# Late branch, one projection for the last head without a block of its own, and the last wavelength on VectorE in every unit but the first

## What is computed

```
for wl in range(16):
    m = cos(phase_modulators[wl])[None, :, None, None]
    scores = einsum('bhqd,bhkd->bhqk', Q * m, K * m) * SCALE
    scores = scores * cos(KERR * scores * scores)
    attn = softmax(scores)
    acc += einsum('bhqk,bhkd->bhqd', attn, V) * interference_weights[wl]
out = x + (acc / 16) @ Wo + bo + experts(layernorm(x))
```

## Time and profile before

| | us |
|---|---|
| median of 3 runs (lowest, highest) | 1777.92 (1775.83, 1778.24) |
| the profiled execution: its own time | 1777.68 |
| the profiled execution: span, first to last instruction | 1776.0 |
| ScalarE busy in the span | 1717.8 (97%) |
| VectorE busy | 1506.6 (85%) |
| TensorE matmuls busy | 1488.9 (84%) |

### The profile page before, as it was taken

How to read it: one execution, slowest core, us unless ns; L and a number is a source line. 1 busy time by engine, 2 the same in 40 slices (tenths; PEclk the granted TensorE clock), 3 DMA queues, 4 the chain that set the end, 5 groups by cost and what they waited for, 6 DMA issues and landing times. The chain is left out here.

```text
span 1776.0 us, 45925 instructions
## 1 busy us (share of the span) xinstructions
PE 1488.9 (84%) x20120; PEld 955.6 (54%) x20120; DVE 1506.6 (85%) x2397; ACT 1717.8 (97%) x524; POOL 166.1 (9%) x184
## 2 busy tenths in 40 slices
PE   5978888887788899999999988878778778778877
PEld 4545555554455566666666655555445545445555
DVE  4555778888988999999999988899998888898784
ACT  3899999999999999999999999999999999999995
POOL 4404000111110000000000000123320000000000
PEclk8999999999999999999999999999999999999999
DMA  3200000110001111011110000000000000000001
GB/s 121 99 15 16 16 5 29 61 43 24 26 9 36 36 43 44 15 33 41 43 43 22 16 18 8 24 25 26 26 21 2 15 15 15 15 15 2 8 13 32
DMA packets 45566, 49.57 MB, mean 28 GB/s; under 512 B 7436, under 2 KB 38068, under 8 KB 45364
## 3 DMA queue, kind: packets, MB, share of 16 engines
q1 hardware_dynamic: 41920, 42.04, 7.4%
q0 software_dynamic: 2048, 4.20, 0.8%
q10 hardware_dynamic: 1396, 0.33, 0.1%
HBM read 30.44 MB, written 15.73 MB: 26 GB/s over the span
## 5 line engine op out<-in xcount | busy, mean ns | idle before, releaser
L1298 ACT ACTIVATE Pr<-T 128x4096 f32<-128x4096 f32 x479 | 1682.6, 3659 | 10.4 <-PE bank L1169 6.6
L1169 PE MATMUL bank<-Pr,Vst 128*32 128x256 f32 x15392 | 932.8, 382 | 257.8 <-ACT Pr L1298 141.3
L1169 PEld LDWEIGHTS bank<-Pr,Vst 128*32 128x32 f32 x15392 | 520.8, 109 | 553.0 <-issue 351.9
L1110 DVE COPY T<-bank 128x512 f32<-128x512 f32 x248 | 168.9, 684 | 73.0 <-PE bank L1104 71.3
L1094 DVE TENSOR_REDUCE negmax<-bank 128x2 f32<-128x512 f32 x248 | 158.6, 679 | 32.9 <-PE bank L1088 32.7
L1262 PE MATMUL bank_b<-terms,ident 128*128 128x128 f32 x1024 | 148.7, 278 | 0.4 <-DVE terms L1250 0.2
L1221 DVE SCALAR_TENSOR_TENSOR shared<-d_mantissa,shared 128x1024 f32<-128x1024 f32 x113 | 142.4, 1260 | 2.6
L1231 DVE TENSOR_SCALAR pv_s<-bank,row_scale 128x512 f32<-128x512 f32 x192 | 142.0, 740 | 0.8 <-PE bank L1169 0.8
L1218 DVE SCALAR_TENSOR_TENSOR shared<-shared,d_scaled 128x1024 f32<-128x1024 f32 x113 | 137.5, 1217 | 0.0
L1215 DVE SCALAR_TENSOR_TENSOR d_mantissa<-d_mantissa 128x1024 f32<-128x1024 f32 x113 | 137.3, 1215 | 0.0
L1262 PEld LDWEIGHTS bank_b<-terms,ident 128*128 128x128 f32 x1024 | 130.0, 191 | 13.5 <-issue 10.7
(11 more groups left out here) (229 smaller groups left out, 900.3 us busy)
## 6 DMA issues: line engine op xcount, KB each, us to landing
Ks<-qk_parts SPq DMA_DIRECT2D x30, 288.0 KB
Qs<-qk_parts SPq DMA_DIRECT2D x90, 96.0 KB
qk_parts<-work SPq DMA_DIRECT2D x12, 384.0 KB, 3.4
work<-in_L_ffn_w_dram SPq DMA_DIRECT2D x16, 256.0 KB, 3.6
dispatched<-d_scaled SPq DMA_DIRECT2D x5, 512.0 KB, 6.4
region<-dispatched SPq DMA_DIRECT2D x8, 320.0 KB, 3.4
expert_out<-work SPq DMA_DIRECT2D x8, 320.0 KB, 2.6
out_dram<-base SPq DMA_DIRECT2D x8, 256.0 KB, 2.2
```

The costliest lines, as they stand in the source:

```text
L1110: nc.vector.tensor_copy(T[par][:, ds(p * BANK, BANK)], sc_bank[rr][:, :]).then_inc(sc_read, 1)
L1169: ins = nc.tensor.matmul(bank[VC * j:VC * (j + 1), half * SEQ:(half + 1) * SEQ], Vst[par][:, at:at + VC], moving, start=opens and half == ...
L1298: nc.scalar.activation(Pr[n % RING][:, :], T[par][:, :], ACT.Exp, scale=scales[u % 2][w]).then_inc(exp_done, 1)
```

## The change

What it does, in four parts.

1. The branch is moved from ahead of `head_*` to after the first scores: normalising, turning, the first Q and K and all of `first_scores` now run ahead of it. The bound uses squares instead of roots, and its operations come later on VectorE and TensorE.
2. Unit 0: one part per step in steps 0 to 3 and two in steps 4 and 5, instead of two ahead of step 0 and two in each of steps 0 to 2; the 16 small matmuls of side 0's gate logits go into four steps; the tiles of unit 1 are scored in steps 6, 7, 9, 10 and transposed 2, 3, 3 in steps 12 to 14.
3. `D_CHUNKS`: four chunks on VectorE in units 1 to 5, where it was 0, 3, 2, 2, 2.
4. The second block is gone. Side 0's heads are projected in unit 30, side 1's first 15 heads (120 rows) in unit 31. The last exp comes in two halves. The last head's 128 x 128 sum, made transposed by exchanging the operands, is multiplied with `spread_rows`, which holds the last 8 rows of `Wo` 16 times on a block diagonal: four matmuls of 512 columns, an add and a store for each.

```diff
-            D_CHUNKS = [{FIRST: 0, NORM: 0, SIDE: 3, ROUTE: 2, QKV: 2, PLAIN: 4, EXPERT: 4, FINAL: 4}[k] for k in KINDS]
+            D_CHUNKS = [{FIRST: 0, NORM: 4, SIDE: 4, ROUTE: 4, QKV: 4, PLAIN: 4, EXPERT: 4, FINAL: 4}[k] for k in KINDS]
...
+            LOGITS0_AT = {(0, 10): 0, (0, 13): 1, (0, 15): 2, (1, 0): 3}
+            PARTS_AT = {0: (0,), 1: (1,), 2: (2,), 3: (3,), 4: (4, 5), 5: (6, 7)}
...
+                if u == 0:
+                    return [(1, 0, p) for p in {6: (0, 1), 7: (2, 3), 9: (4, 5), 10: (6, 7)}.get(w, ())]
...
+                    return [(1, SIDE_B, p) for p in {12: (0, 1), 13: (2, 3, 4), 14: (5, 6, 7)}.get(w, ())]
...
             spread_max(1)
-            pe_v(pe, 1)
             first_transposed(1)
-            pe_v(pe, 2)
-            pe_v(pe, 3)
+            for n in range(1, NQ_SIDE):
+                pe_v(pe, n)
...
+                if (u, w) == LAST_EXP:
+                    for half, signal in enumerate((last_half, exp_done)):
+                        to, src = (t[:, :].rearrange("p (j h k) -> p j h k", j=GR, h=2)[:, :, half, :] for t in (Pr[n % RING], T[par]))
+                        nc.scalar.activation(to, src, ACT.Exp, scale=scales[u % 2][w]).then_inc(signal, 1)
+                    return
...
+            OUT_AT = {(UNITS - 2, 1 + 4 * n + 2 * k): (n, 2 * k) for n in range(NQ_SIDE) for k in range(2)}
+            OUT_AT.update({(UNITS - 1, 5 + 2 * n + k): (NQ_SIDE + n, 2 * k) for n in range(NQ_SIDE) for k in range(2)})
...
+                pe.wait_ge(summed, UNITS)
+                for n in range(NQ_SIDE):
+                    nc.tensor.matmul(last_banks[n][:, :], last_T, spread_rows[:, n * BANK:(n + 1) * BANK], start=True, stop=True).then_inc(o_last, 1)
...
+                sp.wait_ge(spread_room, 1)
+                for j in range(GR):
+                    for q in range(BANK // P):
+                        row, t = (q * GR + j) * HD, q + GR * j
+                        sp.dma_start(spread_rows[row:row + HD, t * D:(t + 1) * D], Wo[D - HD:D, :]).then_inc(rows_spread, 16)
```

More of the change, by code:

```diff
@@ L415, in pre_vector @@
             nc.vector.tensor_copy(flag[:, :], one[:, 1:2]).then_inc(flag_ready, 1)
-        def pre_tensor(pe):
[L418 to L421, removed]
-            ins.then_inc(norms_made, 1)
-            pe.wait_ge(const_ready, 3)
-            pe.wait_ge(bound_ready, 1)
-            nc.tensor.transpose(banks[3][0:1, 0:P], bound[:, 2:3], ident[:, :]).then_inc(bound_turned, 1)
@@ L427, in head_tensor @@
-        def head_tensor(pe):
+            first_max(2)
+            first_max(3)
+            copy_k(3)
+            for b in range(HALF_B, SIDE_B):
+                first_max(b)
+        def pre_tensor(pe):
             def turn_x(n):
@@ L456, in first_scores, with head_tensor @@
                             ins.then_inc(first_made, 1)
+            pe.wait_ge(const_ready, 3)
+            turn_x(0)
+            turn_x(1)
+            pe.wait_ge(first_in, 64)
+            first_qk(0)
+            turn_x(2)
+            pe.wait_ge(w_squared, 2)
+            for i in range(2):
+                ins = nc.tensor.matmul(banks[4][:, i:i + 1], wsq[:, i * D:(i + 1) * D], one_col[:, :], start=True, stop=True)
+            ins.then_inc(norms_made, 1)
+            first_qk(1)
+            first_scores(0)
+            turn_x(3)
+            first_qk(2)
+            pe.wait_ge(bound_ready, 1)
+            first_scores(1)
+            pe.wait_ge(xT_copied, NQ_SIDE)
+            nc.tensor.transpose(banks[6][0:1, 0:P], bound[:, 2:3], ident[:, :]).then_inc(bound_turned, 1)
+            first_qk(3)
+            first_scores(2)
+            first_scores(3)
+        def head_tensor(pe):
             def spread_max(half):
@@ L1148, in pe_products @@
                 pe.wait_ge(v_staged, u + 1)
-                if not shares:
+                if not shares and (u, w) != LAST_EXP:
                     pe.wait_ge(exp_done, EXPS_BEFORE[u] + w + 1)
@@ L1740, in all_general_tensor @@
                     pe_part(pe, m)
-                for i in (GB, LOGITS0):
-                    pe_gate(pe, i)
+                pe_gate(pe, GB)
+                for i in range(4):
+                    pe_logits0(pe, i)
                 for w in range(W):
```

353 lines of the change are left out of this document (177 added, 176 removed).

## The result

The changed kernel is slower: 1786.41 us median of 5 runs (1784.47 to 1789.49) against 1777.5 (1775.83 to 1778.24), ratio 1.0053, 95% interval 1.0043 to 1.0064. The prediction said 1770.1 us, between 1760 and 1777. What came is its rival C. The profiled execution spans 1784.6 us (1776.0 before).

The account below looks back on a forecast made before the run. ScalarE, busy for 97% of the span, was taken as the bound, with VectorE becoming it in units 1 to 5. The terms 0 - 3.3 + 6 - 10.3 = -7.6 against 1777.68 us gave 1770.1 us, range 1760 to 1777.

Parts of the forecast that it names:

- rival C: New units: VectorE and TensorE wait for each other in each; part 3 at +21, sum +7, 1785 us; chance 9%.
- the gaps in part 3's sum: VectorE's idle time in units 1 to 5: about 5 us at unit 1's start, 1 us a unit.
- part 3: Last wavelength of units 1 to 5: VectorE takes 11 chunks more, becomes the bound; 279.8 us against 273.8, +6.
- VectorE's work: Units 1 to 5: 206.35 us before, 278.1 with 11 chunks at 6.5 us and a copy of the logits.
- the busy expert units run nearly without gaps: Reason for taking +6: an expert unit had 1.84 us of VectorE idle time at full load.
- From the last operation to exp 3 of unit 6: Handoff into unit 6: TensorE needs 0.65, 0.6 and 1.9 us before exp 3, due at 10.5.
- +21: Upper bound for units 1 to 5: gaps of 3 us a unit more and the new handoff.
- the 4 x 1.40 of the handoff: Unit boundaries in the upper bound: 1.40 us of waiting at each of 4.
- Part 1: Beginning, late branch: earlier start eaten by TensorE's half clock and VectorE's order; 0, or +1 if the clock falls earlier.
- Part 2: Unit 0: waits of 8.6 us shrink to 5.3; -3.3 us, bounds -6 and 0; unit 1 begins near 104.5.
- Part 4: End: from the last exp to the end 13.1 us instead of 23.4; -10.3, between -6 and -11.5.
- What would show it: Signs: VectorE over 97% busy in units 3 to 5, these over 54 us, ScalarE waiting in steps 2 and 3.

Follow-up runs that it names:

- e1: Changed kernel with the old table of chunks (0, 3, 2, 2, 2 in units 1 to 5): 1769.40 us, 0.9963 of the kernel before.
- e2: Kernel before with only the new table of chunks (four in units 1 to 5): 1794.44 us, 1.0096 of the kernel before.
- e13: Changed kernel with GpSimd's four output-bias additions one by one in units 7, 8, 9 and 18: 1782.27 us, 1.0026 of the kernel before.
- e17: e13 with TensorE kept busy by 24, 20 and 16 constant transposes in the last steps of units 1, 3 and 5: 1781.51 us, one run.
- e6: e1 with VectorE adding the bias to V's second block after the copies of the first T's upper half: 1767.59 us, one run.
- e3: Changed kernel with GpSimd's four output-bias additions moved from unit 1 to unit 7: 1786.17 us, 1.0047 of the kernel before.
- e5: Changed kernel with 24, 20 and 16 constant transposes on TensorE in the last steps of units 1, 3 and 5: 1784.01 us, 1.0041 of the kernel before.

## Why the prediction was wrong

**The step that failed: the gaps in part 3's sum, and with them its "+6 against 273.8".** Part 3 measured +19.05 and so turned the sign; with the other terms as they came (-10.4) the kernel would have been faster with anything up to +10.4 here. The mechanism was that of the forecast (VectorE becomes the bound, TensorE waits for it, ScalarE for TensorE), and e1 and e2 show that nothing else in the change makes the loss. VectorE's time from unit 1's begin to the end of the last operation on unit 5's chunks, in the changed kernel, in e13 and in e17 (stretch, us; VectorE busy; clock):

```profile
403.20 1.22 DVE L1238 SCALAR_TENSOR_TENSOR shared<-d_mantissa,shared 128x1024 f32<-128x1024 f32 x1
...
106.03:404.35 298.32, 282.61 (x474) 0.96 0.08 27
...
106.50:401.76 295.26, 276.59 (x474) 0.97 0.08 27
...
106.88:400.86 293.98, 276.60 (x474) 0.99 0.08 27
```

By the forecast's own terms, which had 287 us here (288 less the 1 behind the last operation), 277 of it work:

- *VectorE's work.* 282.6 us, of which 5.9 is what the three held-up operations took too much. The load itself, 276.7, was right, and with it the 6.5 us a chunk. The 5.9, GpSimd's hold on VectorE, was put at nothing without a reason.
- *Gaps*, 5 at unit 1's start and 1 a unit, 10 in all. The first was right (5.2). The second came as 10.5 and not 5 in the changed kernel, together 15.7; with GpSimd out of the way (e13) all gaps are 18.7, and with the clock kept up too (e17) 17.4. This is the term taken too small: "the busy expert units run nearly without gaps" was carried over to units that ask for more than there is. An expert unit asks for less than ScalarE gives, so a delay in it is absorbed; here every delay adds. The largest ones in e13 behind unit 1 are 3.27 and 2.49 us, where VectorE's first chunk operation of units 2 and 3 waits for TensorE's products.
- *From the last operation to exp 3 of unit 6*, 3.15 forecast. It took 5.05, with products at the lower clock (3.64 and 2.64 us); 3.2 in e17.

Together 11.3 + 1.9 = 13.2, the +6 made +19. In e17, where GpSimd and the lower clock are taken away, the sum is the forecast's +6, 7.4 more of gaps and 0.5 less of work, 12.9; its M is 12.8 above the kernel before. So by causes the runs divide the 19.05 into 4.4 for GpSimd (e13), 1.8 for the clock that shows only with GpSimd out of the way (e17), and 12.8 of overload: the +6 that was forecast and 7 of gaps that were not. Which wait between VectorE and TensorE makes how much of these gaps was not isolated.

**What the profile before could have told.** GpSimd's additions stood in it at 160.31 to 169.70, in a stretch in which VectorE did little that they could disturb, and the forecast looked at GpSimd not at all: it asked what VectorE's new operations cost, not what they do to an engine beside it, nor where that engine's next work then falls.

Rival C named the right place and nearly the right price, but as an upper bound at 9%. Its +21 is 6 and 5 x 3 us of gaps; the 4 x 1.40 of the handoff named beside them are not in it, and with them it would be 26.6.

**Part 1 (0): right.** The upper half's exps began at 47.27 (48.0 forecast, 47.96 before), after 2.79 us of idle time as said, and the clock was at 0.50 from 31 to 47 us, in which TensorE was busy for 14.8 of the 16. The order on VectorE did delay them by 2.6 us (e6); whether unit 1's begin hangs on it is open.

**Part 2 (-3.3, unit 1 at 104.5): right in kind.** Unit 0 waited 7.1 us (8.6 before, 5.3 forecast), and the wait for unit 1's second half was there, 3.6 us for the forecast 2. Unit 1 began at 106.03. But this number varies: over the 16 other profiles with this beginning (e6's differs in one place) it lay between 102.8 and 108.7, so a single profile can't test a term of 3 us, and the -1.9 above is partly luck of the two profiles. The waits named in the forecast, 0.7, 2 and 2, make 4.7, not the 5.3 it put down.

**Part 4 (-10.3): -8.5.** From the last exp to the end 14.9 us, 13.1 forecast. The products after the last exp took 2.65 instead of 1.2, since TensorE was still at VectorE's wavelength; store and exit took 4.2 (1780.41 to 1784.6) instead of 3.6; the matmuls 3.7 instead of 4.1.

**"What would show it"** held for units 4 and 5 (98% and 99% busy, 58.5 and 56.3 us long, waits in steps 2 and 3). Unit 3 lasted only 53.0 (93% busy): VectorE had done some 5 us of that unit's work within the long unit 2 (63.4 us busy there, for 51.8 and the 5.9 above).

## What to carry to other kernels

An engine at 97% that never waits is the bound, but the second engine's room has to be counted stage by stage: work moved to it paid here up to 51.8 us in stages of 52.7 to 53.7, and cost from 55 on. Above that line each gap and each late handoff adds in full, so that gaps read from a stage with room are too small (1 us a unit taken, 2 to 3 measured). Before an engine is loaded, read what GpSimd does in the same stretch: it is slowed itself, and its later work may fall on the one short operation that everything waits for. Where the start of a stretch varies by some us from run to run, compare from a fixed event inside it.

## What was not expected of the hardware

- GpSimd holds VectorE up by whole operations. Beside GpSimd's 128x1024 additions (2.35 us each where nothing held them) a `TENSOR_TENSOR` on 128x16 took 2.3 us for 0.18, a `CAST` 2.3 for 0.17, a `SCALAR_TENSOR_TENSOR` on 128x1024 2.9 for 1.2; `TENSOR_REDUCE` and `RECIPROCAL` from a bank beside them kept their 1.28 and 0.44. The Trainium skill (SBUF — State Buffer, Who interferes with whom) says that a VectorE instruction with two inputs in SBUF contends with a GpSimd instruction that reads SBUF, that a cast can contend in a mode with two ports, that the one then fully blocks for the whole instruction of the other, and that a `TENSOR_REDUCE` never contends on this chip. The traces agree.
- In e3 one VectorE operation waited for all four additions in a row (10.70 us), while in the changed kernel each waited for one. What decides between the two no run here shows.
- The other way round VectorE's chunks stretched GpSimd's 16 normalisations from 12.5 us (no chunk in unit 1) to 15.8 (two) and 20.9 (four).
- TensorE's granted clock was 0.50 after idle time of 3.6 us at 165, of 3.0 at 281 and of 2.3 at 397, and 24, 20 and 16 transposes of a constant in these gaps kept it at 1.00 (e5, where it fell in unit 2 after 4.5 us of idle time instead).
- In the 17 traces with the new beginning 4.8 to 6.5 us passed from the issue of unit 0's last pair of stores to the load that waits for them. With the first exp, at 38.7 to 41.2, this moves the begin of unit 1 from run to run.
